# A selective-scan block on one core: dt as fp32 broadcast into the decay tile by DMA, two-step exponentials, a third PSUM bank

## What is computed

```
xn = layernorm(x)
# branch 1
xp   = rmsnorm(xn) @ in_proj_W;  x_z, z = split(xp)          # E = 256 each
xc   = silu(conv1d(x_z, 4 taps, per channel) + conv_b)
dt   = clip(softplus(xc @ dt_W + dt_b), 0.001, 0.1)          # (B, T, 256)
Bp   = xc @ B_W;  Cp = xc @ C_W                              # (B, T, 64)
A    = -exp(A_log)                                           # 64 values
for t in range(512):                                         # h: (B, 256, 64)
    h = exp(dt_t * A) * h + dt_t * B_t * xc_t
    y_t = sum over the 64 states of h * C_t
x1   = xn + (y * silu(z)) @ out_proj_W
out1 = x1 + (silu(n2 @ gate_W) * (n2 @ up_W)) @ down_W       # n2 = rmsnorm(x1)
# branch 2: three dense layers with weights of +1 and -1 on [xn, -xn], relu between
```

## Time and profile before

| | |
|---|---|
| median of three runs | 1300.1 us |
| profiled execution, its own time | 1294.7 us |
| its span, first to last instruction | 1292.7 us |
| PE, DVE, ACT, POOL busy | 89%, 81%, 81%, 67% of the span |
| moved by DMA | 56.5 MB, mean 44 GB/s |
| scan steps 1 to 512 (start of L1147) | 219.9 to 1262.7 us |

### The profile page before, as it was taken

How to read it: one execution, slowest core, us unless ns; L and a number is a source line. 1 busy time by engine, 2 the same in 40 slices (tenths; PEclk the granted TensorE clock), 3 DMA queues, 4 the chain that set the end, 5 groups by cost and what they waited for, 6 DMA issues and landing times.

```text
span 1292.7 us, 34025 instructions
## 1 busy us (share of the span) xinstructions
PE 1152.1 (89%) x10152; PEld 514.8 (40%) x10152; DVE 1050.2 (81%) x2254; ACT 1041.8 (81%) x1748; POOL 861.5 (67%) x1220
## 2 busy tenths in 40 slices
PE   4999973888999999999999999999999999898998
PEld 2666651223343334343433343434343434343435
DVE  3578773878888888888888888888888888888884
ACT  1666663879888888888888888888888888888891
POOL 5355443767777777777777767676767676777771
PEclk9898975769999999999999999999999999999999
DMA  4022334111111111111111111111111111111100
GB/s 122 33 102 100 102 120 130 44 27 30 32 35 33 32 35 33 32 32 31 33 33 33 33 33 33 33 33 33 33 33 33 33 33 33 33 33 33 34 6 9
DMA packets 73848, 56.50 MB, mean 44 GB/s; under 512 B 43968, under 2 KB 63296, under 8 KB 70720
## 3 DMA queue, kind: packets, MB, share of 16 engines
q1 hardware_dynamic: 73792, 55.80, 14.5%
HBM read 36.38 MB, written 19.40 MB: 43 GB/s over the span
## 4 chain that ended last, share of the span: by engine, by line
PE 45%; DVE 16%; issue 10%; ACT 4%; POOL 4%; DVEq 1%; ACTq 0%; POOLq 0%
PE ps L961 14%; PE ps L867 9%; PE ps L873 7%; PE ps L1056 7%; DVE state L1156 6%; DVE ps L1147 5%; PE ps L1070 4%; POOL decayed L812 3%; ACT state L1109 2%; PE ps L1021 2%; DVE c_cols L1192 2%; DVE n L1255 1%; DVE y_tok L1201 1%; PE ps L1034 1%; ACT square L1124 1%
## 5 line engine op out<-in xcount | busy, mean ns | idle before, releaser
L812 POOL TENSOR_TENSOR decayed<-decay,state 128x256 f32<-128x256 f32 x1024 | 727.4, 731 | 279.7 <-DVE state L1156 259.2
L1097 ACT ACTIVATE decay<-ps,a_col 128x512 f32<-128x512 f32 x1024 | 704.8, 693 | 100.1 <-PE ps L867 67.1
L1147 DVE TENSOR_TENSOR ps<-decay,ps 128x512 f32<-128x512 f32 x512 | 354.7, 693 | 111.9 <-ACT state L1109 81.1
L867 PE MATMUL ps<-moving,dt_pick 48*128 48x256 bf16 x2048 | 404.4, 279 | 30.7 <-DVE state L1156 20.9
L1156 DVE TENSOR_TENSOR state<-decayed,ps 128x256 f32<-128x256 f32 x1024 | 392.4, 416 | 28.7 <-POOL decayed L812 10.0
L961 PE MATMUL ps<-state,c_cols 128*32 128x256 f32 x4096 | 335.1, 400 | 0.0
L1109 ACT COPY state<-ps 128x512 f32<-128x512 f32 x512 | 297.4, 581 | 32.8 <-DVE ps L1147 30.5
L873 PE MATMUL ps<-moving,b_rows 48*128 48x256 bf16 x1024 | 201.7, 278 | 66.2 <-DVE ps L1147 65.0
L867 PEld LDWEIGHTS ps<-moving,dt_pick 48*128 48x128 bf16 x2048 | 115.3, 94 | 244.9 <-issue 219.5
L880 PE MATMUL ps<-moving,b_rows 48*128 48x256 bf16 x1024 | 203.4, 279 | 0.0
L1056 PE MATMUL ps<-h,w 128*128 128x256 f32 x512 | 172.4, 422 | 1.0 <-DVE h L1281 0.8
(11 more groups left out here) (122 smaller groups left out, 1004.1 us busy)
## 6 DMA issues: line engine op xcount, KB each, us to landing
moving<-u_stage SPq DMA_DIRECT2D x64, 288.0 KB
moving<-dt_stage SPq DMA_DIRECT2D x64, 96.0 KB
b_stage<-b_parts SPq DMA_DIRECT2D x24, 192.0 KB, 2.7
b_rows<-b_stage SPq DMA_DIRECT2D x256, 18.0 KB
dt_stage<-dt_parts SPq DMA_DIRECT2D x8, 512.0 KB, 2.8
u_stage<-u_parts SPq DMA_DIRECT2D x8, 512.0 KB, 3.2
dt_stage<-dt_parts SPq DMA_DIRECT2D x8, 256.0 KB, 2.1
u_stage<-u_parts SPq DMA_DIRECT2D x8, 256.0 KB, 2.4
```

The source lines that it names most:

```text
L812: nc.gpsimd.tensor_tensor(decayed[:, p], decay[:, k % RING, p * E:(p + 1) * E], state[:, (k - 1) % RING, p * E:(p + 1) * E], ALU.mult).the ...
L867: return nc.tensor.matmul(ps[:, DTP + f, p * E:(p + 1) * E], dt_pick[rows(f), p, :], moving[rows(f), cb, kk, :], start=True, stop=True)
L1097: nc.scalar.activation(decay[:, k % RING, f * SELF:(f + 1) * SELF], ps[:, DTP + f, :], ACT.Exp, scale=a_col[:, 2:3]).then_inc(ready, 1)
L1147: nc.vector.tensor_tensor(ps[:, ACCP + k % 2, :], decay[:, k % RING, SELF:QE], ps[:, ACCP + (k - 1) % 2, :], ALU.mult).then_inc(acc_decaye ...
```

## The change

- **dt.** `dt_tok` (fp32, now double-buffered) is stored as it is to an fp32 `dt_stage` of shape (2, Q, T, E). The bf16 split of dt, `dt_pick` and the pick matmuls are gone. `load_dt` loads four steps with two DMAs, one per half of the partitions: each copies 4 rows of 4 KB (four steps x 256 channels, one row per pair of batches) to each of 64 partitions, straight into the decay tile. There are three such tiles of four steps.
- **Exponential.** ACT takes it in place, once for two steps (4 x 512 columns), then does two copies of the acc half.
- **PSUM.** The two freed banks go to a third acc bank (`acc_copied` of t-3 gates L1147) and a second bank for the self product. The contraction lags by 3 steps.
- **PE order.** Per step: accumulate of k and self product of k+1 in turn, contract of k-3, finishing.
- **B with C.** One matmul gives C and B in feature form; B's token form comes from four transposes, which wait for the ACT copy. B's parts are padded with zeros to 128 columns, stored by one DMA, and loaded in rows of 4 KB whose source has an inner broadcast of 3 (36 KB per DMA, eight per chunk).
- **Split of u.** The two subtractions move from DVE to POOL, in the place of those of dt.
- **SP.** Loads are written out step by step: dt of four steps is loaded when the block of four that used its slot is done; u and B are put between.
- `gate`, `k0_f` and the weights share or give back memory. The loop body covers 96 steps instead of 32.

```diff
-    LAG = 2
+    LAG = 3
+    TS = 4
+    NDEC = 3
+    NACC = 3
-    dt_stage = nc.dram_tensor("dt_stage", (2, NP, HALF, T, E), BF16, kind="Internal").ap()
-    b_stage = nc.dram_tensor("b_stage", (NP, NP, B, T, N), BF16, kind="Internal").ap()
+    dt_stage = nc.dram_tensor("dt_stage", (2, Q, T, E), F32, kind="Internal").ap()
+    b_stage = nc.dram_tensor("b_stage", (NP, B, T, 2 * N), BF16, kind="Internal").ap()
...
+                        wait_all(sp, [(S["dt_ready"], n + 1)])
+                        sp.dma_start(dt_stage[bb, q].rearrange("(p j) e -> p (j e)", j=NJ),
+                                     dt_tok[:, bb].rearrange("p j e -> p (j e)")
+                                     ).then_inc(S[f"dt_stored{bb}"], 16)
                         for parts, stage, i0, i1, ready in (
-                                [(dt_parts, dt_stage[n // HALF], 0, 2, "dt_mid_ready"),
-                                 (u_parts, u_stage[n // HALF], 0, 2, "u_mid_ready"),
-                                 (dt_parts, dt_stage[n // HALF], 2, 3, "dt_split"),
-                                 (u_parts, u_stage[n // HALF], 2, 3, "u_split")]
-                                + [(b_parts, b_stage[:, i], 0, NP, "b_split") for i in range(NP)]):
+                                (u_parts, u_stage[n // HALF], 0, 2, "u_mid_ready"),
+                                (b_parts, b_stage, 0, NP, "b_split"),
+                                (u_parts, u_stage[n // HALF], 2, 3, "u_split")):
...
-                            m = nc.tensor.matmul(ps[bb * N:(bb + 1) * N, CB, :], w_c[:, h, :], xc_feat[:, bb, h, :],
+                            m = nc.tensor.matmul(ps[:, CB, :], w_cb[:, h, bb, :], xc_feat[:, bb, h, :],
...
                         after(pe, "z_ready", n)
+                        after(pe, "c_ready", n)
+                        b_half = slice((1 - bb) * N, (2 - bb) * N)
                         for j in range(NJ):
-                            for h in range(EH):
-                                m = nc.tensor.matmul(ps[:, BT, j * N:(j + 1) * N],
-                                                     xc_feat[:, bb, h, j:T:NJ], w_dtb[:, h, E:E + N],
-                                                     start=(h == 0), stop=(h == EH - 1))
+                            m = nc.tensor.transpose(
+                                ps[:, BT, j * N:(j + 1) * N],
+                                cb_feat[b_half, bb, bass.ds(q, 1), j:T:NJ].rearrange("n o t -> n (o t)"),
+                                ident[b_half, b_half])
...
+            decay = pb("decay", [P, NDEC, Q, TS, E])
...
+                    def load_dt(t, slot, waits):
+                        wait_all(sp, waits)
+                        for bb in range(2):
+                            sp.dma_start(decay[bb * N:(bb + 1) * N, slot].rearrange("n q t e -> n q (t e)"),
+                                         dt_stage[bb, :, bass.ds(t, TS), :].rearrange("q t e -> q (t e)")
+                                         .unsqueeze(0).broadcast_to([N, Q, TS * E])
+                                         ).then_inc(dt_loaded[slot], 16)
...
+                    def load_b(t, cb, batch):
+                        for b in batch:
+                            r0 = (b // HALF) * HROW
+                            sp.dma_start(b_rows[r0 + b % HALF:r0 + UROWS:HALF, cb, (b // 2) % HQ]
+                                         .rearrange("r t n -> r (t n)"),
+                                         b_stage[:, b, bass.ds(t, TC), :].rearrange("j t n -> j (t n)")
+                                         .unsqueeze(1).broadcast_to([NP, NP, TC * P])
+                                         ).then_inc(b_loaded[cb], 16)
...
+                        def next_dt(kc, waiting=True):
+                            used = t0 + kc * TS
+                            load_dt(t0 + (kc + 2) * TS, (m * BTS + kc + 2) % NDEC,
+                                    [(self_state[1], used)] if waiting else [])
...
+                            load_u(t0 + TC, 1, [(acc_state, t0 + 1)])
+                            load_b(t0 + TC, 1, range(0, 2))
+                        next_dt(1)
+                            load_b(t0 + TC, 1, range(2, 5))
+                            store(i - 2)
+                        wait_all(sp, [(self_state[1], t0 + 2 * TS)])
+                            load_b(t0 + TC, 1, range(5, B))
+                        next_dt(2, False)
+                        next_dt(3)
+                        next_dt(4)
+                            load_u(t0 + STEPS, 0, [(acc_state, t0 + TC + 1)])
+                            load_b(t0 + STEPS, 0, range(0, 2))
+                        next_dt(5)
+                        load_tokens(i)
+                            load_b(t0 + STEPS, 0, range(2, 5))
+                        next_dt(6)
+                            load_b(t0 + STEPS, 0, range(5, B))
+                        next_dt(7)
+                        next_dt(8)
...
+                    def products(i, k, m):
+                        t = i * STEPS + k
+                        ahead = not (known(t) and t + 1 >= T)
+                        if ahead:
+                            wait_chunk(i, k + 1)
+                            wait_step(pe, self_state[1], t - 1)
                         wait_step(pe, acc_decayed, t)
                         for p in range(HQ):
+                            acc = acc_matmul(m, k, p)
...
+                            if ahead:
+                                own = self_matmul(k + 1, p)
...
+                        if ts == 0:
+                            act.wait_ge(dt_loaded[slot], dec_loads(m, r, k) * (16 * 2))
+                        pair = decay[:, slot, :, ts:ts + 2, :].rearrange("p q t e -> p q (t e)")
+                        nc.scalar.activation(pair, pair, ACT.Exp, scale=a_col[:, 2:3]).then_inc(decay_ready, 1)
...
+                        if k % 2 == 0:
+                            exp_decay(i, k + 2, m, r)
+                            copy_state(i, k - 2, m)
+                            copy_state(i, k - 1, m)
...
-                        wait_step(dve, acc_copied, t - 2)
+                        wait_step(dve, acc_copied, t - NACC)
```

More of the change, by code:

```diff
@@ L52, in mamba_and_binary_mlp_block @@
     STEPS = 2 * TC
-    LAG = 2
+    LAG = 3
+    TS = 4
+    NDEC = 3
+    NACC = 3
+    BTS = STEPS // TS
+    CYCLE = 3
+    assert CYCLE * BTS % NDEC == 0 and CYCLE * STEPS % NACC == 0
     TG = STEPS
@@ L556, in dt_and_u @@
                         after(dve, "dt0_ready", n)
-                        after(dve, "dt_r1_ready", n, back=1)
-                        nc.vector.tensor_scalar(dt_tok[:], soft[:, 0], DT_MIN, DT_MAX, ALU.max, ALU.min
+                        if not (isinstance(q, int) and q == 0):
+                            dve.wait_ge(S[f"dt_stored{bb}"], q * 16)
+                        nc.vector.tensor_scalar(dt_tok[:, bb], soft[:, 0], DT_MIN, DT_MAX, ALU.max, ALU.min
                                                 ).then_inc(S["dt_ready"], 1)
@@ L727, in chunks, with acc_bank, dec_slot, dec_loads @@
                     for k in range(STEPS):
-                        body(i, k)
-                with eng.Fori(3, BODIES - 1) as i:
-                    for k in range(STEPS):
-                        body(i, k)
-                for k in range(STEPS):
-                    body(BODIES - 1, k)
+                        body(i, k, i, 0)
+                with eng.Fori(1, (BODIES - 1) // CYCLE) as r:
+                    for m in range(CYCLE):
+                        for k in range(STEPS):
+                            body(r * CYCLE + m, k, m, r)
+                for k in range(STEPS):
+                    body(BODIES - 1, k, (BODIES - 1) % CYCLE, (BODIES - 1) // CYCLE)
+            def acc_bank(m, k):
+                return ACCP + (m * STEPS + k) % NACC
+            def dec_slot(m, k):
+                return (m * BTS + k // TS) % NDEC
+            def dec_loads(m, r, k):
+                return r * (CYCLE * BTS // NDEC) + (m * BTS + k // TS) // NDEC + 1
             def known(t):
@@ L746, in _, with load_u @@
                 def _(sp):
-                    def load(t, cb):
+                    def load_dt(t, slot, waits):
[5 more added lines that the diff above has]
+                                         ).then_inc(dt_loaded[slot], 16)
+                    def load_u(t, cb, waits):
+                        wait_all(sp, waits)
                         for f in range(2):
@@ L780, in store @@
                                          ).then_inc(G["f_stored"], 16)
-                    def body(i):
-                        if not (known(i) and i < 3):
-                            store(i - 3)
-                        for cb in range(2):
-                            wait_all(sp, [(acc_state, i * STEPS + (cb + 1) * TC - STEPS + 1)])
-                            load(i * STEPS + cb * TC, cb)
-                            if cb == 0:
-                                load_tokens(i - 1)
-                    body(1)
@@ L798, in _ @@
```

(36 more changed lines are left out.)

281 lines of the change are left out of this document (110 added, 171 removed).

## The result

The changed kernel takes 2099.2 us (median of four runs, 2095.4 to 2101.6). The kernel before took 1312.6 in the runs beside them (median of four, 1293.9 to 1327.3). The ratio is 1.618, with a 95% interval of 1.610 to 1.626; it leaves out the executions of the kernel before that fell in its slower state, and so stands against about 1297 us. The forecast was 1486, in a range of 1230 to 1610: slower was foreseen, by 186 us over the 1300 of then, and it became 799.

The account below looks back on a forecast made before the run. Slow dt loads by DMA were to bound the changed kernel: 190 us before the first load, 128 blocks of 9.8 (1254), 11 after the last block and 29 at the end gave 1484 of span, 1486 of time; range 1230 to 1610.

Parts of the forecast that it names:

- The exponential: ACT in the scan: one exponential of 2048 columns for two steps takes 1.91 us, 0.96 a step instead of 1.39.
- the wait for the copy: DVE's wait ahead of L1147 for ACT's acc copy, 0.15 us a step, goes with the third acc bank.
- Rival 2: Scan bound by DVE: full-rate dt loads, B on nine engines, dt never late; 1186 us; chance 0.08.
- the signs named: Signs of a right forecast: ACT idle before the exponential, DVE and ACT below 75%, DMA share near 0.9 at 240 GB/s.
- 13.4 GB/s per engine: Rate taken for the scan's dt loads: 16 engines give 214 GB/s, 9.8 us a block, 2.45 us a step.
- my two traits: Reasons for slow dt loads: many engines writing a narrow run of partitions, and staged rows a power of two apart.
- In the forecast it is covered by the other 13 engines' slow dt loads: Scan loads: u and B, on about three engines, add nothing to the 9.8 us of a dt block.
- rival 3: Half-rate dt plus uncovered u and B on three engines, 51.3 us per 16 steps, up to 1870 us; chance 0.08.
- the queue never empties: Scan's DMA queue: three dt blocks asked for ahead, so 128 blocks follow each other at 9.8 us, 1254 us.
- Rival 1: Scan bound by three engines with u and B, dt at full rate; 1224 to 1275, say 1250 us; chance 0.26.
- The turning point: Scan's dt loads: above 24 GB/s per engine the kernel is no slower than before, below it slower.
- Rival 5: PE's clock at 1.2 GHz for half of the scan's time; 1519 us; chance 0.04.

Follow-up runs that it names:

- e4: Changed kernel without the dt loads after the first three blocks (decay values differ): 1230.2 us.
- e16: e11 with each dt block asked for once the exponentials have read its slot, not when the state's last step is done: 1212.1 us, ratio 0.936 to before.
- e15: e12 without u and B: 1222.5 us.
- e14: Changed kernel without the loads of u and B after the first chunks of 16 steps: 1615.6 us.
- e2: Changed kernel with the four rows of each dt load all read from one row: 2082.7 us.
- e7: Changed kernel with dt staged eight times, one 2 MB DMA per block, 16 rows of 16 KB each to 8 adjacent partitions: 1911.0 us.
- e12: e7 with a 16 KB source row of its own for each of the 128 partitions (dt values differ): 1477.8 us.
- e3: Changed kernel with u loaded by three DMAs and B from three staged copies, on 12 and 9 engines instead of 3: 1825.0 us.
- e1: Changed kernel with each of a block's two dt loads writing all 128 partitions from two rows (wrong dt for half the batches): 1525.6 us.
- e10: Changed kernel with dt rounded to 16-bit floats, loaded into a tile of its own; the exponential writes fp32 decay elsewhere: 1484.6 us.
- e11: e10 with u and B spread over more engines as in e3: 1287.5 us, ratio 0.990 to the kernel before.
- e6: Changed kernel with the two 64-partition halves of a dt block issued from two queues, SP's and ACT's: 2029.2 us.

## Why the prediction was right or wrong

**Right: what the engines gain.** The exponential (2.008 us measured, 1.91 taken), the wait for the copy (0.19 a step, 0.15 taken) and stage 1 (17.07 us a batch, 17.1 taken) are near what was worked out, and PE without its picks is busy 1.69 us a step in e4, at a granted clock of 0.93, where 1.56 was taken at 1.00; the first dt load is issued at 178.06 us, 27 us before the first of the scan's loads in the earlier trace rows, where I had 15. DVE-bound steps of 1.85 us are 1.90 in e4 and e16. Rival 2 was the right picture of the engines: its 1186 stands beside 1222 (e15) and 1212 (e16). Of the signs named, ACT's idle before the exponential and DVE and ACT below 75% came out; a DMA share near 0.9 at 240 GB/s did not (0.79 at 162), and that is the sign of what failed.

**Right: half rate, and why it was to be suspected.** The step that took 13.4 GB/s per engine from the earlier trace rows held: packets of 4 KB in 331 ns are 12.4, and e14's full engines give 209 GB/s against 214 taken. The reason that I gave, four rows a power of two apart, is refuted by e2. The narrow destination is the one of my two traits that stayed; e7 shows that 128 partitions alone do not mend it, and that how they fall to the engines decides is argued from e12.

**Wrong: "In the forecast it is covered by the other 13 engines' slow dt loads".** This is the step that failed. The three engines that carry u and B have a full share of slow dt loads of their own. I had the sum for it myself, in rival 3: 39.1 us of dt and 12.1 of the rest per 16 steps, 51.3 at the least. Cover would have needed other engines to take over their dt packets, and the trace shows the contrary: five packets or fewer in flight in 422 of 1700 us, and in 24 of 1400 once u and B are spread (e3). Measured: 58.5 us per 16 steps. e14 puts a price on all of u and B: 2099 - 1616 = 483 us, 15.1 per 16 steps. e3 splits it: 2099 - 1825 = 274 us are the crowding on three engines, and 1825 - 1616 = 209 us are what u and B cost when spread over engines that are full at half rate. Their 28.3 MB at e3's 190 GB/s make 149 of these, an estimate, and most of the rest is the lower mean rate, against 197 in e14 from 200 to 1583 us. The 613 us over the forecast are these 483 and the 130 of the next step.

**Wrong: "the queue never empties".** With u and B it empties for most engines, as said. e14 has none of them, keeps a share of 0.98 from 300 to 1500 us, and still takes 1616, 130 above the sum. 128 blocks at 10.0 us instead of 9.8 are 26 of that. From 178 to 300 us the DMA engines moved 159 GB/s instead of 209, since the first u and B loads held three engines and SP stood behind them: 29. The three holes are 36. Tokens and results, 4.2 MB at 209 GB/s, are 20 that the sum left out. Against these the first load went out at 178, 12 us before the sum's 190, so some 30 us stay without a name. These are readings of the slices, not experiments of their own.

**Mis-sized: rival 3.** It took u and B at 25.6 GB/s per engine. While all engines work u's packets take 652 ns instead of 312, 12.6 GB/s. So 12.1 us became part half rate, and its 1870 was 229 short. With 8 in 100 on it, and the range ending at 1610, it was priced far too low: nothing in the rows spoke for cover, and a transfer pinned to certain engines adds to what else is pinned there.

**Rival 1** is e12 and e1: full rate and three engines with u and B. It took 1250; they take 1478 and 1526, 39 to 41 us per 16 steps against 31 to 32.6. Its packets of u, too, take 544 ns at full load (e1). The turning point that I gave, 24 GB/s per engine for dt, was too low a bar: e1's dt packets ran at 25.6 and it is slower than before by 17%. **Rival 5**, the clock: in e4 and e16 the clock over the scan (210 to 1180 us) is 0.88 and 0.91 and the steps from 300 us on are 1.90, so it costs little; in the changed kernel it is 0.65, with PE busy in 60% of the time and waiting for the rest, so I take it for a consequence and no cause. No run tests that by itself.

## What to carry to other kernels

Add up a DMA-bound loop per engine, not per byte: a transfer that only uses three engines adds its whole time to those three, and where each block is asked for only when an earlier one is used up, the other thirteen wait with them (274 us here). Before a broadcast load replaces compute, look for a load of its very shape (partitions, rows, how many partitions a row goes to) in a trace with all engines busy; its rate can be half of what other loads of the same packet size reach. When a load is late, ask what its slot really waits for: once dt had a tile of its own (e10, e11), its last reader was the exponential, and naming that instead of the state was worth 6% (e16 against e11). In the changed kernel, where the exponential is taken in place, the multiplies read the slot last and this is not to be had.

## What the runs showed of the hardware that I had not expected

- One DMA over all 128 partitions is no warrant for full rate: 16 rows to 8 adjacent partitions each took 1247 ns per 16 KB packet, 128 rows of their own 614, alone both 613 (e7, e12). e12 reads one small region over and over, e7 all of it; that this made the difference is not excluded by a run of its own, but e1 read all of its region at full rate. The Trainium skill, SBUF — State Buffer, "Can I just issue two DMAs to hit both halves?", says that one transfer over 128 partitions is the only way to all ports; e7 is one and runs at half rate all the same.
- The slow form is slow only in company: a 4 KB packet took 161 ns with one to three in flight and 331 with 14 or more (changed kernel). A probe with one small load would not have shown it.
- Two halves of the partitions on two queues gained 3% (e6). The Trainium skill, SBUF — State Buffer, "Can I just issue two DMAs to hit both halves?", has 6% for two at once over a single one; the run agrees that it is no remedy.
- An issue of dt holds SP for 0.64 us in the median and for up to 10.76, one of 36 KB of B for up to 11.90 (changed kernel). A row of merged issues also holds the waits between them, so its length alone does not show that SP was held.
- A hole of about 12 us in the DMA traffic comes once in each turn of the loop (e14, 743, 1003 and 1266 us); around the first, DVE is idle for 7.8 and 6.3 us (until 737 and 745 us) with nothing that the profile shows to wait for.
